# Mamba stage of a decoder: GpSimd takes seven of the 32 products with C, z of batch 1 later, no spare products in the items

## The chip, the cores and the metric

One Trainium2 chip, one core of it. The metric is the device time of one execution in microseconds (us), median of the runs. Engines: TensorE (PE; PEld is its weight load), VectorE (DVE), ScalarE (ACT), GpSimd (POOL), SyncE (SP, which here only issues DMAs).

## What is computed

A decoder layer: a Mamba block, a mixture of experts, a cross-attention, six layers of local attention with feed-forward, and a last norm. The change touches only the Mamba block (B = 2, L = 512, 256 channels, 16 states):

```python
xz = rmsnorm(x) @ in_proj_w
xi, z = split(xz)
xi = silu(causal_conv4(xi) + conv_b)
dbc = xi @ x_proj_w                       # 64 for the step size, 16 for B, 16 for C
delta = softplus(dbc[..., :64] @ dt_proj_w + dt_proj_b)
Bm, Cm = dbc[..., 64:80], dbc[..., 80:96]
A = -exp(A_log)
h = exp(delta * A) * h + (delta * xi) * Bm     # for each of 16 states, along L
y = sum over states of h * Cm
y = (y + D_skip * xi) * silu(z)
out = y @ out_proj_w                      # and the residual is added
```

## The kernel before

**Layout.** Channels lie on the 128 partitions in two halves k = 0, 1; time lies along the free axis. All is fp32. After a front part (norm, convolution as four accumulated products, low-rank projection, step size of batch 0), `build_mamba` works through 32 *items*, item i = 16 b + n being state n of batch b. Every engine has its own written-out program for the items, and semaphores tie them together.

**One item.** SP loads B's row, broadcast to 128 partitions, from DRAM into a ring of four (`b_rows`, L158), once GpSimd has used the row four items earlier. GpSimd multiplies u = delta * x by it (`dbx`, 128x1024, a ring of three, L492), at most three items ahead of the scans. ScalarE makes the decay exp(delta * A) for each half into one of four PSUM banks (`decay`, L315), each once the scan two items back has read its bank. VectorE scans each half (`scan`, L412) into `state` (two buffers), and multiplies the state by C's row (`times_c`, L419, 128x1024) into `hc`, a ring of three. Its order is scan(i, 0), times_c(i - 1), scan(i, 1). TensorE spreads C's row over the partitions by a product with a selection matrix into one PSUM bank (`spread_c`, L194), and adds `hc` into the sum banks by products with the identity (`add_state`, L205). spread_c(i + 1) stands ahead of add_state(i); it waits until times_c(i) has read the bank, and two spare products (`busy`, L170, bf16 zeros) run ahead of it.

**What is threaded between the items.** For batch 1: TensorE's products for z10 and z11 (`gate_proj`, L178) after items 0 and 1, with ScalarE copying x10, x11 (`raw`, L294) after the decays of item 1 and z10, z11 after those of items 2 and 3. x1's SiLU (`activated`, L333 to L341, with a table load before and one after) follows the decays of item 3. Then the low-rank product (`low_rank`, L183) ahead of item 4, rank copy and low part on VectorE (items 6, 7), step size products (items 7, 11), softplus in three ScalarE steps (items 10 to 14), delta on VectorE (`step_sizes`, L404, items 10, 13), u on GpSimd (`step_times_x`, L475, ahead of items 12 and 16). For batch 0: SiLU of z (item 16), skip on VectorE (L423, item 17), gate on GpSimd (L497, item 19), output product (item 20), residual (L427, item 22). Batch 1 ends the same way on VectorE after item 31.

The banks 3 (SPARE), 4 and 5 (the two sums) and 7 (C's row) are shared between these uses. A single bank serves z10, z11, the low-rank product, the step sizes and the output product.

## Time and profile before

| | us |
|---|---|
| median of 3 runs (lowest to highest) | 1226.83 (1225.7 to 1227.47) |
| the profiled execution | 1222.83 |
| its span | 1221.0 |
| busy: PE, DVE, ACT, POOL | 1126.8, 943.2, 845.5, 653.3 |

The page's shares are averages over all stages. The Mamba stage is the first eighth of the span: it ends with the last residual at 158.29 us. In the order of time, a line gives start, length, engine, line of the kernel, what is written from what, and in brackets how long the engine was idle before it and what ended that. The granted clock is TensorE's, 1.00 for 2.4 GHz and 0.50 for 1.2 GHz.

### The profile page before, as it was taken

To read this page: it belongs to the slowest core of one execution; us is meant where nothing else is said; L and a number is where in the kernel's file an instruction comes from. 1 tells how busy PE (TensorE), PEld (TensorE's weight loads), DVE (VectorE), ACT (ScalarE), POOL (GpSimd) and SP (SyncE) were. 2 spreads that over 40 slices of the span, in tenths; PEclk is the share of its full clock that TensorE was granted. 3 is DMA by queue.
4 is the path that set the end of the run, shared out by engine and by line. 5 is a ranking of instruction groups with operands and counts; after the bars stand their busy time and mean duration, and the time that the engine had idled before them with its cause. 6 is when DMAs were issued, how large, how long until landed. Compare 5 with 4: busy or idle time off the path is not lost. (4 is left out here: it accounts for less than half of the span.)

```text
span 1221.0 us, 26331 instructions
## 1 busy us (share of the span) xinstructions
PE 1126.8 (92%) x9600; PEld 718.5 (59%) x9700; DVE 943.2 (77%) x1386; ACT 845.5 (69%) x1344; POOL 653.3 (54%) x527
## 2 busy tenths in 40 slices
PE   9788879999776999999999999999999999999975
PEld 3223248787333766666666676666666666667641
DVE  4699957778455878887888787888888788878843
ACT  5446356665353788688877788688877887787844
POOL 2567424543334765655656566656666565756510
PEclk9899979999886999999999999999999999999998
DMA  4222035100202453345435353445334443534310
GB/s 154 78 61 78 26 54 216 52 26 1 103 1 52 111 156 93 102 118 135 100 96 135 105 127 94 119 104 142 98 100 120 123 122 80 127 94 123 92 52 17
DMA packets 80183, 115.58 MB, mean 95 GB/s; under 512 B 25891, under 2 KB 32482, under 8 KB 79674
## 3 DMA queue, kind: packets, MB, share of 16 engines
q1 hardware_dynamic: 79546, 113.13, 35.0%
q8 instruction: 77, 1.26, 0.4%
q10 hardware_dynamic: 512, 0.80, 0.2%
q14 instruction: 48, 0.39, 0.1%
HBM read 39.28 MB, written 0.66 MB: 33 GB/s over the span
## 5 line engine op out<-in xcount | busy, mean ns | idle before, releaser
L1758 POOL TENSOR_TENSOR st_sq_sum<-h 128x512 f32<-128x512 f32 x96 | 122.2, 1272 | 222.9 <-ACT h L1515 222.2
L1762 POOL TENSOR_TENSOR mo_w<-mo_w,x 128x512 f32<-128x512 f32 x96 | 122.7, 1278 | 101.7 <-DVE x L1633 101.7
L1647 DVE SCALAR_TENSOR_TENSOR st_turned<-banks,mo_w 128x1024 f32<-128x1024 f32 x96 | 117.5, 1224 | 73.0 <-ACT banks L1526 40.7
L1515 ACT ACTIVATE h<-banks 128x512 f32<-128x512 f32 x192 | 114.6, 597 | 70.3 <-PE banks L1358 65.9
L1419 PEld LDWEIGHTS banks<-st_p_blocks,st_vs 128*64 128x64 f32 x1536 | 81.4, 137 | 78.1 <-issue 76.0
L1378 PEld LDWEIGHTS banks<-st_wv,stream 128*128 128x128 f32 x768 | 100.7, 191 | 45.2 <-issue 44.4
L1764 POOL TENSOR_TENSOR mo_w<-mo_w,x 128x512 f32<-128x512 f32 x96 | 122.4, 1275 | 0.0
L1547 ACT ACTIVATE st_p_blocks<-banks 64x512 f32<-64x512 f32 x192 | 112.0, 583 | 3.2 <-PE banks L1407 0.8
L1366 PE MATMUL banks<-st_sq_sum,head_ones 128*128 128x512 f32 x192 | 101.4, 610 | 11.9 <-POOL st_sq_sum L1758 7.7
L1771 POOL TENSOR_TENSOR mo_w<-st_prob,st_ri 128x512 f32<-128x512 f32 x96 | 100.3, 1045 | 15.0 <-DVE st_ri L1733 15.0
L1395 PE MATMUL banks<-st_k_blocks,st_qT 128*32 128x128 f32 x3072 | 104.6, 277 | 1.6 <-DMA st_k_blocks<-st_turned 1.5
L1419 PE MATMUL banks<-st_p_blocks,st_vs 128*64 128x64 f32 x1536 | 99.4, 227 | 6.1 <-ACT st_p_blocks L1547 5.5
L1522 ACT ACTIVATE st_rn<-banks,fill 128x512 f32<-128x512 f32 x96 | 65.8, 685 | 55.5 <-PE banks L1366 55.2
L1378 PE MATMUL banks<-st_wv,stream 128*128 128x128 f32 x768 | 101.2, 275 | 0.0
L1429 PE MATMUL banks<-x,st_wo 128*128 128x512 f32 x192 | 99.3, 599 | 1.8 <-ACT x L1540 1.7
L1354 PE MATMUL banks<-st_y_high,st_w_high 128*128 128x512 f32 x192 | 92.0, 479 | 9.4 <-PEq L1885 4.8
L1419 PE MATMUL banks<-st_p_blocks,st_vn 128*64 128x64 f32 x1536 | 95.7, 222 | 0.0
L1395 PEld LDWEIGHTS banks<-st_k_blocks,st_qT 128*32 128x32 f32 x3072 | 78.6, 110 | 25.9 <-issue 17.4
L492 POOL TENSOR_TENSOR ma_dbx<-ma_u,ma_b_rows 128x1024 f32<-128x1024 f32 x31 | 72.7, 2362 | 28.6 <-DVE ma_state L412 28.5
L1581 ACT ACTIVATE st_prob<-st_prob 128x512 f32<-128x512 f32 x96 | 60.3, 628 | 39.2 <-DVE st_prob L1711 38.4
L412 DVE TENSOR_TENSOR_SCAN ma_state<-banks,ma_dbx 128x512 f32<-128x512 f32 x64 | 75.6, 1207 | 8.4 <-ACT banks L315 6.6
L1419 PEld LDWEIGHTS banks<-st_p_blocks,st_vn 128*64 128x64 f32 x1536 | 81.9, 138 | 0.0
(240 smaller groups left out, 2713.3 us busy)
## 6 DMA issues: line engine op xcount, KB each, us to landing
st_qT<-st_turned SPq DMA_DIRECT2D x192, 128.0 KB, 2.3
st_k_blocks<-st_turned SPq DMA_DIRECT2D x384, 64.0 KB, 2.0
st_vs<-st_vn SPq DMA_DIRECT2D x96, 192.0 KB, 2.5
ma_b_rows<-state_rows SPq DMA_DIRECT2D x32, 256.0 KB, 3.1
st_w_raw<-in_w_qk SPq DMA_DIRECT2D x12, 512.0 KB, 4.9
st_vs<-st_vn SPq DMA_DIRECT2D x96, 48.0 KB, 2.1
mo_w_all<-gate_rows SPq DMA_DIRECT2D x1, 3072.0 KB, 11.8
st_wv<-in_w_v SPq DMA_DIRECT2D x12, 256.0 KB, 2.9
```

The lines of the kernel that those rows point to most:

```text
L1366: mm(NORM_BANK, C["head_ones"], sq_sum[:], start=True, stop=True).then_inc(norm_done.sem, 1)
L1378: last = mm(V_BANK[:, rows], Y[:, b, rows], wv[:, pair, :], start=True, stop=True)
L1395: last = mm(SCORE_BANK[rows].rearrange("p (o h i k) -> p o h i k", o=2, h=2, i=2)[:, odd, :, i, :], qT[:, r, pair, t0:t0 + WIN], k_blocks[ ...
L1419: last = mm(TURN_BANK[rows, P * j:P * j + P].rearrange("p (h o q) -> p h o q", h=2, q=WIN)[:, :, odd, :], (vn if odd else vs)[:, r, j, row ...
L1429: mm(OUT_BANK[b], wo[:, pair, :], oT[:, n % 2, :], start=(pair == 0), stop=(pair == 7)).then_inc(wo_step.sem, 1)
L1515: A(sq[:, part, :], ps[:, part, :], ACT.Square).then_inc(sq_done.sem, 1)
L1547: A(p_blocks[rows, r, half, :], TURN_BANK[rows, :], ACT.Copy).then_inc(pt_copied.sem, 1)
L1647: v.scalar_tensor_tensor(turned[:, h % 4], NORM_BANK.unsqueeze(1).to_broadcast([P, 2, SEQ]), 1e12, cos_part[:, which], ALU.min, ALU.mult). ...
L1758: nc.gpsimd.tensor_tensor(sq_sum[:], sq[:, 0, :], sq[:, 1, :], ALU.add).then_inc(sq_summed.sem, 1)
L1762: nc.gpsimd.tensor_tensor(cos_part[:, which, 0, :], cos_part[:, which, 0, :], sin_part[:, 1, :], ALU.subtract).then_inc(add_done.sem, 1)
L1764: nc.gpsimd.tensor_tensor(cos_part[:, which, 1, :], cos_part[:, which, 1, :], sin_part[:, 0, :], ALU.add).then_inc(add_done.sem, 1)
L1771: nc.gpsimd.tensor_tensor(pn[:, r], prob[:, r], ri[:, r, :].unsqueeze(2).to_broadcast([P, 8, 64]), ALU.mult).then_inc(pn_done.sem, 1)
```

## The change

Seven items, 2, 6, ..., 26 (`BY_POOL`), have their product with C on GpSimd, from SBUF: C's row comes by DMA into the one buffer `c_rows`. For this all 32 rows (B and C) go out to DRAM. GpSimd does the product of item m after dbx of item m + 2. TensorE spreads no C row for these items, and `add_state` and the scans wait for whichever engine made the product (`hc_at`). `state` gets a third buffer, so that scan(i) waits for the product of item i - 3. TensorE's two spare products per item are gone, and ten stand ahead of item 0 instead. The products for z10 and z11 move from items 0 and 1 to 15 and 18, their copies to the decays of items 17 and 20. x1's SiLU, the low-rank product and what follows from it for batch 1 come one item earlier. SiLU of z0 one item earlier, of z1 one later, output product and residual of batch 0 two later. `mag` is no longer separate per batch.

```diff
--- before.py
+++ after.py
@@ -99,14 +99,15 @@
     xc = sb("xc", [P, 2, 2, SEQ])
     dt = sb("dt", [DT_RANK + 1, 2, SEQ])
     bc2 = sb("bc2", [P, 2, SEQ], F32R)
-    mag = sb("mag", [P, 2, 2, SEQ])
+    mag = sb("mag", [P, 2, SEQ])
     delta = sb("delta", [P, 2, 2, SEQ])
     u = sb("u", [P, 2, 2, SEQ])
     still = sb("still", [P, SEQ], BF16)
     a_neg = sb("a_neg", [P, 2, STATES])
     b_rows = sb("b_rows", [P, B_RING, SEQ])
     dbx = sb("dbx", [P, 3, 2, SEQ])
-    state = sb("state", [P, 2, 2, SEQ])
+    state = sb("state", [P, 3, 2, SEQ])
+    c_rows = sb("c_rows", [P, SEQ])
     hc = sb("hc", [P, 3, 2, SEQ])
     gated = sb("gated", [P, 2, 2, SEQ])
 
@@ -122,11 +123,19 @@
     b_flat_done, b_out, b_in = flow("b_flat_done"), flow("b_out"), [flow(f"b_in_{i}") for i in range(B_RING)]
     c_done, decay_done, dbx_done, scan_done, hc_done, sum_done = (flow(n) for n in (
         "c_done", "decay_done", "dbx_done", "scan_done", "hc_done", "sum_done"))
+    pool_hc_done, c_in = flow("pool_hc_done"), flow("c_in")
     gate_step, out_done, h1_done = flow("gate_step"), flow("out_done"), flow("h1_done")
 
     block = ctx.enter_context(nc.Block())
 
     ITEMS = 2 * STATES
+
+    BY_POOL = range(2, ITEMS - 2, 4)
+    BY_DVE = [i for i in range(ITEMS) if i not in BY_POOL]
+
+    def hc_at(i):
+
+        return (pool_hc_done.sem, BY_POOL.index(i) + 1) if i in BY_POOL else (hc_done.sem, BY_DVE.index(i) + 1)
 
     FRONT = {name: i + 1 for i, name in enumerate(("x00", "x01", "z00", "z01", "x10", "x11", "z10", "z11"))}
     RAW = {name: i + 1 for i, name in enumerate(("z00", "z01", "x10", "x11", "z10", "z11"))}
@@ -151,11 +160,16 @@
             b, n = divmod(i, STATES)
             if n == 0:
                 sp.wait_ge(b_flat_done.sem, b + 1)
-                sp.dma_start(d["states"][b], b_flat[64:64 + STATES, b, :]).then_inc(b_out.sem, 16)
+                sp.dma_start(d["states"][b], b_flat[64:64 + 2 * STATES, b, :]).then_inc(b_out.sem, 16)
                 sp.wait_ge(b_out.sem, 16 * (b + 1))
             if i >= B_RING:
                 sp.wait_ge(dbx_done.sem, 2 * (i - B_RING + 1))
-            sp.dma_start(b_rows[:, i % B_RING, :], bass.AP(d["states"].tensor, i * SEQ, [[0, P], [1, SEQ]])).then_inc(b_in[i % B_RING].sem, 16)
+            sp.dma_start(b_rows[:, i % B_RING, :], bass.AP(d["states"].tensor, (2 * STATES * b + n) * SEQ, [[0, P], [1, SEQ]])).then_inc(b_in[i % B_RING].sem, 16)
+            if i in BY_POOL:
+                at = BY_POOL.index(i)
+                if at >= 1:
+                    sp.wait_ge(pool_hc_done.sem, at)
+                sp.dma_start(c_rows[:], bass.AP(d["states"].tensor, (2 * STATES * b + STATES + n) * SEQ, [[0, P], [1, SEQ]])).then_inc(c_in.sem, 16)
 
     @block.tensor
     def _(pe):
@@ -188,14 +202,15 @@
 
         def spread_c(i):
             b, n = divmod(i, STATES)
+            if i in BY_POOL:
+                return
             if i > 0:
-                pe.wait_ge(hc_done.sem, i)
-                busy(2)
+                pe.wait_ge(hc_done.sem, BY_DVE.index(i))
             mm(ps[:, C_BANK, :], select[64:128, n, :], bc2[64:128, b, :], start=True, stop=True).then_inc(c_done.sem, 1)
 
         def add_state(i):
             b, n = divmod(i, STATES)
-            pe.wait_ge(hc_done.sem, i + 1)
+            pe.wait_ge(*hc_at(i))
             if n == 0:
                 if b == 0:
                     pe.wait_ge(raw_done.sem, RAW["x11"])
@@ -239,27 +254,33 @@
         convolved(1, 1)
         pe.wait_ge(C["const_in"].sem, C["const_n"])
         pe.wait_ge(out_in.sem, 16)
+        pe.wait_ge(raw_done.sem, RAW["z01"])
+        for _ in range(10):
+            mm(ps[:, SUM + 1, :], still[:, 0:P], still[:], start=True, stop=True)
         for i in range(ITEMS):
-            if i == 4:
-                pe.wait_ge(raw_done.sem, RAW["z11"])
+            if i == 3:
+                pe.wait_ge(raw_done.sem, RAW["x10"])
                 low_rank(1, SPARE)
-            if i == 7:
+            if i == 6:
                 pe.wait_ge(dt_copied.sem, 2)
                 pe.wait_ge(low_done.sem, 2)
                 pe.wait_ge(b_flat_done.sem, 2)
                 step_size(1, 0, SPARE)
-            if i == 11:
+            if i == 10:
                 pe.wait_ge(delta_done.sem, 3)
                 step_size(1, 1, SPARE)
-            if i == STATES + 4:
+            if i == 15:
                 pe.wait_ge(delta_done.sem, 4)
+                gate_proj(1, 0)
+            if i == 18:
+                pe.wait_ge(raw_done.sem, RAW["z10"])
+                gate_proj(1, 1)
+            if i == 22:
+                pe.wait_ge(raw_done.sem, RAW["z11"])
                 out_proj(0)
             if i + 1 < ITEMS:
                 spread_c(i + 1)
             add_state(i)
-            if i in (0, 1):
-                pe.wait_ge(raw_done.sem, RAW[("x10", "z10")[i]])
-                gate_proj(1, i)
         pe.wait_ge(h1_done.sem, 1)
         out_proj(1)
 
@@ -298,7 +319,7 @@
             A(bc2[64:128, b, :], ps[64:128, bank, :], ACT.Copy).then_inc(high_done.sem, 1)
 
         def flat(b, bank):
-            A(b_flat[64:64 + STATES, b, :], ps[64:64 + STATES, bank, :], ACT.Copy).then_inc(b_flat_done.sem, 1)
+            A(b_flat[64:64 + 2 * STATES, b, :], ps[64:64 + 2 * STATES, bank, :], ACT.Copy).then_inc(b_flat_done.sem, 1)
 
         def decay(i):
             b, n = divmod(i, STATES)
@@ -319,15 +340,15 @@
 
         def magnitude(b, k):
             ac.wait_ge(dtp_done.sem, 2 * b + k + 1)
-            A(mag[:, b, k, :], ps[:, SPARE if b else k, :], ACT.Abs).then_inc(softplus_step.sem, 1)
+            A(mag[:, k, :], ps[:, SPARE if b else k, :], ACT.Abs).then_inc(softplus_step.sem, 1)
 
         def decline(b, k):
             ac.wait_ge(softplus_step.sem, STEP[b, k, "abs"])
-            A(mag[:, b, k, :], mag[:, b, k, :], ACT.Exp, scale=-1.0).then_inc(softplus_step.sem, 1)
+            A(mag[:, k, :], mag[:, k, :], ACT.Exp, scale=-1.0).then_inc(softplus_step.sem, 1)
 
         def log_of(b, k):
             ac.wait_ge(softplus_step.sem, STEP[b, k, "exp"])
-            A(mag[:, b, k, :], mag[:, b, k, :], ACT.Ln, bias=C["one"]).then_inc(softplus_step.sem, 1)
+            A(mag[:, k, :], mag[:, k, :], ACT.Ln, bias=C["one"]).then_inc(softplus_step.sem, 1)
 
         def activated(which, at):
             nc.scalar.preload_act_table_set("silu_and_others")
@@ -357,21 +378,21 @@
             if i == 1:
                 raw("x10")
                 raw("x11")
-            if i in (2, 3):
-                raw(("z10", "z11")[i - 2])
-            if i == 3:
+            if i == 2:
                 activated("x1", "x11")
-            if i == 7:
+            if i == 6:
                 high(1, SPARE)
                 flat(1, SPARE)
+            if i in (9, 12):
+                magnitude(1, i // 12)
+                decline(1, i // 12)
             if i in (10, 13):
-                magnitude(1, i // 13)
-                decline(1, i // 13)
-            if i in (11, 14):
-                log_of(1, i // 14)
-            if i == 16:
+                log_of(1, i // 13)
+            if i == 15:
                 activated("z0", "z01")
-            if i == 23:
+            if i in (17, 20):
+                raw(("z10", "z11")[i // 20])
+            if i == 24:
                 activated("z1", "z11")
 
     @block.vector
@@ -401,22 +422,22 @@
 
         def step_sizes(b, k):
             dv.wait_ge(softplus_step.sem, (4, 6, 9, 12)[2 * b + k])
-            v.scalar_tensor_tensor(delta[:, b, k, :], ps[:, SPARE if b else k, :], 0.0, mag[:, b, k, :], ALU.max, ALU.add).then_inc(delta_done.sem, 1)
+            v.scalar_tensor_tensor(delta[:, b, k, :], ps[:, SPARE if b else k, :], 0.0, mag[:, k, :], ALU.max, ALU.add).then_inc(delta_done.sem, 1)
 
         def scan(i, k):
             j = 2 * i + k
             dv.wait_ge(decay_done.sem, j + 1)
             dv.wait_ge(dbx_done.sem, 2 * i + (k + 1 if i == 0 else 2))
-            if i >= 2:
-                dv.wait_ge(hc_done.sem, i - 1)
-            v.tensor_tensor_scan(state[:, i % 2, k, :], ps[:, DECAY[j % 4], :], dbx[:, i % 3, k, :], 0.0, ALU.mult, ALU.add).then_inc(scan_done.sem, 1)
+            if i >= 3:
+                dv.wait_ge(*hc_at(i - 3))
+            v.tensor_tensor_scan(state[:, i % 3, k, :], ps[:, DECAY[j % 4], :], dbx[:, i % 3, k, :], 0.0, ALU.mult, ALU.add).then_inc(scan_done.sem, 1)
 
         def times_c(i):
             dv.wait_ge(scan_done.sem, 2 * i + 2)
-            dv.wait_ge(c_done.sem, i + 1)
+            dv.wait_ge(c_done.sem, BY_DVE.index(i) + 1)
             if i >= 3:
                 dv.wait_ge(sum_done.sem, 2 * (i - 2))
-            v.tensor_tensor(hc[:, i % 3], state[:, i % 2], ps[:, C_BANK, :].unsqueeze(1).to_broadcast([P, 2, SEQ]), ALU.mult).then_inc(hc_done.sem, 1)
+            v.tensor_tensor(hc[:, i % 3], state[:, i % 3], ps[:, C_BANK, :].unsqueeze(1).to_broadcast([P, 2, SEQ]), ALU.mult).then_inc(hc_done.sem, 1)
 
         def skip(b, k):
             dv.wait_ge(sum_done.sem, 2 * STATES * (b + 1) - 1 + k)
@@ -437,21 +458,21 @@
             v.tensor_tensor(u[:, 0, k, :], delta[:, 0, k, :], xc[:, 0, k, :], ALU.mult).then_inc(u_done.sem, 1)
         for i in range(ITEMS):
             scan(i, 0)
-            if i >= 1:
+            if i >= 1 and i - 1 in BY_DVE:
                 times_c(i - 1)
             scan(i, 1)
+            if i == 5:
+                rank_copy(1, SPARE)
             if i == 6:
-                rank_copy(1, SPARE)
-            if i == 7:
                 low_part(1, SPARE)
-            if i == 10:
+            if i == 9:
                 step_sizes(1, 0)
-            if i == 13:
+            if i == 12:
                 step_sizes(1, 1)
             if i == STATES + 1:
                 for k in range(2):
                     skip(0, k)
-            if i == STATES + 6:
+            if i == STATES + 8:
                 residual(0)
         times_c(ITEMS - 1)
         for k in range(2):
@@ -476,10 +497,11 @@
 
         for i in range(ITEMS):
             b, n = divmod(i, STATES)
-            if i == 12:
+            if i == 11:
                 step_times_x(0)
-            if i == 16:
+            if i == 15:
                 step_times_x(1)
+            if i == STATES:
                 pool.wait_ge(u_done.sem, 4)
             pool.wait_ge(b_in[i % B_RING].sem, 16 * (i // B_RING + 1))
             if i >= 3:
@@ -490,6 +512,13 @@
                     nc.gpsimd.tensor_tensor(dbx[:, 0, k, :], u[:, 0, k, :], b_rows[:, 0, :], ALU.mult).then_inc(dbx_done.sem, 1)
             else:
                 nc.gpsimd.tensor_tensor(dbx[:, i % 3], u[:, b], b_rows[:, i % B_RING, :].unsqueeze(1).to_broadcast([P, 2, SEQ]), ALU.mult).then_inc(dbx_done.sem, 2)
+            if i - 2 in BY_POOL:
+                at, m = BY_POOL.index(i - 2), i - 2
+                pool.wait_ge(scan_done.sem, 2 * m + 2)
+                pool.wait_ge(c_in.sem, 16 * (at + 1))
+                if m >= 3:
+                    pool.wait_ge(sum_done.sem, 2 * (m - 2))
+                nc.gpsimd.tensor_tensor(hc[:, m % 3], state[:, m % 3], c_rows[:].unsqueeze(1).to_broadcast([P, 2, SEQ]), ALU.mult).then_inc(pool_hc_done.sem, 1)
             if i == STATES + 3:
                 pool.wait_ge(gate_step.sem, 2)
                 pool.wait_ge(silu_done.sem, 5)
@@ -1834,7 +1863,7 @@
 
 
     d = {**d, "line": nc.dram_tensor("bias_line", (HEADS, SPAN), F32).ap(),
-         "states": nc.dram_tensor("state_rows", (BATCH, STATES, SEQ), F32).ap(),
+         "states": nc.dram_tensor("state_rows", (BATCH, 2 * STATES, SEQ), F32).ap(),
          "gates": nc.dram_tensor("gate_rows", (EXPERTS, BATCH, SEQ), F32).ap()}
     with ExitStack() as ctx:
         def sb(name, shape, dt=F32):
```

## Rows read from the trace of the kernel before

**Rows 1.** Mamba by stretch: PE, PEld, DVE, ACT, POOL busy us, granted clock, DMA share, GB/s

```profile
48.00:60.00 12.00, 8.98 (x17) 3.45 (x18) 8.74 (x8) 6.75 (x11) 4.71 (x2) 0.72 0.20 58
84.00:96.00 12.00, 9.93 (x24) 3.60 (x25) 12.00 (x13) 8.52 (x11) 10.48 (x6) 1.00 0.29 97
```

**Rows 2.** Groups by line, 20 to 170 us: busy us, mean ns, idle before

```profile
L412 DVE TENSOR_TENSOR_SCAN ma_state<-banks,ma_dbx 128x512 f32<-128x512 f32 x64 | 75.6, 1207 | 8.4 <-ACT banks L315 6.6 <-POOL ma_dbx L492 1.5 <-POOL ma_dbx L490 0.3
...
L315 ACT ACTIVATE banks<-ma_delta,ma_a_neg 128x512 f32<-128x512 f32 x64 | 43.2, 686 | 43.3 <-DVE ma_state L412 43.0 <-DVE ma_delta L404 0.2
L419 DVE TENSOR_TENSOR ma_hc<-ma_state,banks 128x1024 f32<-128x1024 f32 x32 | 38.2, 1195 | 2.7 <-issue 2.6
```

**Rows 3.** VectorE in order of time: start, length, instruction, idle before it

```profile
40.93 1.22 DVE L412 TENSOR_TENSOR_SCAN ma_state<-banks,ma_dbx 128x512 f32<-128x512 f32 x1 [2.39 <-ACT banks L315]
...
48.62 1.22 DVE L412 TENSOR_TENSOR_SCAN ma_state<-banks,ma_dbx 128x512 f32<-128x512 f32 x1 [4.22 <-ACT banks L315]
...
59.20 1.22 DVE L419 TENSOR_TENSOR ma_hc<-ma_state,banks 128x1024 f32<-128x1024 f32 x1 [2.64 <-issue]
...
132.75 2.33 DVE L412 TENSOR_TENSOR_SCAN ma_state<-banks,ma_dbx 128x512 f32<-128x512 f32 x2
135.00 1.19 DVE L419 TENSOR_TENSOR ma_hc<-ma_state,banks 128x1024 f32<-128x1024 f32 x1
```

**Rows 4.** ScalarE in order of time, the same columns

```profile
31.67 1.29 ACT L315 ACTIVATE banks<-ma_delta,ma_a_neg 128x512 f32<-128x512 f32 x2
39.72 0.60 ACT L294 ACTIVATE ma_sz<-banks 128x512 f32<-128x512 f32 x1 [6.75 <-PE banks L178]
...
43.96 1.28 ACT L333 ACT_TABLE_LOAD   x1
45.25 1.33 ACT L337 ACTIVATE ma_xc<-ma_xc,ma_chan 128x512 f32<-128x512 f32 x2
```

**Rows 5.** TensorE in order of time, the same columns

```profile
34.41 0.38 PE L170 MATMUL banks<-ma_still 128*128 128x512 bf16 x1 [3.27 <-DVE ma_hc L419]
...
51.02 1.03 PE L170 MATMUL banks<-ma_still 128*128 128x512 bf16 x2 [4.74 <-DVE ma_hc L419]
51.98 0.79 PE L194 MATMUL banks<-ma_bc,ma_select 64*128 64x512 f32 x1
52.70 3.78 PE L205 MATMUL banks<-ma_hc,ident 128*128 128x512 f32 x4
56.28 1.97 PE L183 MATMUL banks<-ma_xc,ma_proj_w 128*128 128x512 f32 x4
58.08 0.59 PE L170 MATMUL banks<-ma_still 128*128 128x512 bf16 x2
...
72.97 1.98 PE L205 MATMUL banks<-ma_hc,ident 128*128 128x512 f32 x4
```

**Rows 6.** GpSimd in order of time, the same columns

```profile
29.26 9.30 POOL L492 TENSOR_TENSOR ma_dbx<-ma_u,ma_b_rows 128x1024 f32<-128x1024 f32 x4
...
103.02 2.50 POOL L497 TENSOR_TENSOR ma_gated<-ma_gated,ma_sz 128x512 f32<-128x512 f32 x2 [2.21 <-DVE ma_gated L423]
...
140.85 2.36 POOL L492 TENSOR_TENSOR ma_dbx<-ma_u,ma_b_rows 128x1024 f32<-128x1024 f32 x1 [1.00 <-DVE ma_state L412]
```

**Rows 7.** VectorE in order of time, its other work: step size, skips

```profile
76.37 0.66 DVE L404 SCALAR_TENSOR_TENSOR ma_delta<-banks,ma_mag 128x512 f32<-128x512 f32 x1
...
101.57 1.38 DVE L423 SCALAR_TENSOR_TENSOR ma_gated<-ma_xc,ma_chan,banks 128x512 f32<-128x512 f32 x2
...
153.53 0.75 DVE L423 SCALAR_TENSOR_TENSOR ma_gated<-ma_xc,ma_chan,banks 128x512 f32<-128x512 f32 x1 [1.49 <-PE banks L205]
```

**Rows 8.** DMA of the B rows: burst at 22.9 us, then 83 to 140 us

```profile
DMA to landing us min/median/max: 3.1/3.8/4.2
...
DMA to landing us min/median/max: 3.0/3.1/3.3
```

**Rows 9.** TensorE in a later stretch: busy us, granted clock, DMA, GB/s

```profile
315.00:321.00 6.00, 3.11 (x6) 1.00 0.00 0
```

## The prediction

> **What bounds the kernel now.** I began with the table of busy time by stage. Only the Mamba stage, to 158.3 us of a 1221.0 us span, contains lines of the diff. In it VectorE is busy 12.00 of 12.00 us from 84 us on, but 8.74 of 12.00 us from 48 to 60 us [rows 1]. The groups by line say what fills it: 64 scans (1207 ns) and 32 products with C (1195 ns) [rows 2]. VectorE's order of time gives the pace: two scans start at 132.75 and the product at 135.00, though their record is 2.33 long, so a scan holds VectorE for 1.125 us and a record ends 0.085 after the next instruction may start; the product of 1.19 then holds it for 1.11, and an item, two scans and a product, takes 3.36 us [rows 3]. The three holes are in the same view: idle 2.39 us before 40.93, 4.22 before 48.62 and 2.64 before 59.20. Each is counted from the record's end, 0.085 late, so the holes cost 9.25 + 0.25 = 9.5 us [rows 3]. ScalarE's order of time explains two: it sits 6.75 us waiting for TensorE's z10 product before it may copy z10, and the decays of item 3 queue behind; then z11's copy, a table load of 1.28, two SiLUs of 1.33 together and a table load of 1.28 all stand ahead of the decays of item 4 [rows 4]. The third is TensorE's: at half clock C's row takes 0.72 us and two sum products 3.58, from start to start (51.98, 52.70, 56.28), then the low-rank product and two spare products stand ahead of C's row for item 5 [rows 5]. GpSimd isn't the bound: 2.36 us of work, 1.00 us of waiting in an item; four without a wait take 9.30, 2.33 from start to start [rows 6].
>
> **The change, part by part.** "Item" is a pair (batch, state), 0 to 31.
>
> *Products moved.* Items 2, 6, ..., 26, seven of the 32, lose VectorE's product: 7 x 1.11 = 7.8 us off VectorE's path. Each puts one 128x1024 product of two SBUF operands on GpSimd, for which I take that of its own product dbx, 2.36 us (2.33 from start to start) [rows 6]. Bounds: no reason makes it shorter; slower I can't see from this trace, since the type, shape and kinds of operands are the same.
>
> *Holes at the front.* z10 and z11 leave items 0 to 3 of TensorE and ScalarE, and the SiLU of x1 moves ahead by one item. Laid out anew: decays of item 2 end at 33.0 as now [rows 4]; load, two SiLUs, load take 3.9, to 36.9; decay of item 3 is there at 37.6, and VectorE wants it at 38.45 (40.93 less the hole of 2.48). So both ScalarE holes go; margin 0.85. The third goes with the second, whose 4.74 us of idle TensorE stand ahead of the half clock [rows 5]. What is late next is, first, TensorE: the product with C of item 2 on GpSimd starts when dbx of item 4 is done (38.6 as now [rows 6]) and ends at 41.0, the two sums then take 1.83 (1.98 at full clock, less the overlap of 0.2 that the slow ones show [rows 5]), the low-rank product, four passes of the same form, 1.8, and C's row of item 4 some 0.45: 45.1, and VectorE wants it at 45.1. No margin, even with TensorE at full clock. Second GpSimd: dbx of item 5 ends at 43.3, wanted at 44.0. So 9.5 us go, with 0 to 0.5 coming back here.
>
> *GpSimd's queue later.* Over four items GpSimd has 5 x 2.33 = 11.65, VectorE 8 x 1.125 + 3 x 1.11 = 12.33, so GpSimd keeps up by 0.7 only, and every other thing on it is felt. It waits for the new step size before item 11 and from then on works without a pause. From dbx 11 to dbx 13 it then has dbx, product, dbx = 6.99, while VectorE needs four scans, one product and a step size of 0.6 [rows 7] = 6.2: a stall of 0.75. From 13 to 17 GpSimd has 5 x 2.33 + 1.23 for u = 12.9 against 12.33: 0.55. From 17 to 21 it has 11.65 + 2.46 for the gate [rows 6] and 0.2 of waiting for the first skip, 14.3, against 12.33 + 1.3 for the two skips [rows 7]: 0.65. After that VectorE is the slower one again. Together +1.95 us. Bounds 1 to 4: it is a difference of nearly equal sums, and 0.1 us more per GpSimd instruction would already be 2 us over the 20 in a row.
>
> *C's row by DMA.* Seven transfers of 256 KB are queued on SP between the B rows, and from item 6 on SP waits for the last GpSimd product with C. Behind that wait stand the B rows of the next two items, in a burst of three. A single B row lands in 3.0 to 3.2 us; of the burst of four at the start the last takes 4.2 [rows 8]. The B row of item 7 is issued at 41.5, so it lands by 45.6 at the latest, and GpSimd wants it at 45.6; that of items 19 and 23 has the same margin. Cost 0, at most 0.3 each for three, under 1 us. The first transfer out carries 32 rows of 2 KB in place of 16. The nearest rows are those of 256 KB in 3.1 us; a transfer 32 KB longer should land within 0.3 us of the old one. Taken as 0, since the first scan waits for VectorE's own u, bounds -0.1 to +0.3.
>
> *Spare products removed.* TensorE loses two per item. At the end C's row for item 31 no longer has 0.53 of them ahead of it, so the last sums start as soon as their product is there: the 1.49 us wait before the skip [rows 7] becomes 1.05: -0.45. What the removal does to TensorE's clock is a rival below. Ten spare products before the loop fill 31.1 to 33.3, where TensorE is idle for 3.27 us [rows 5]: free.
>
> *Hidden, each with its cover.* z10 and z11 later (TensorE has about 1 us free in an item, ScalarE the 3.36 less two decays of 0.69 [rows 2]); the smaller magnitude buffer (its two users are far apart); the third state buffer (GpSimd's product is done 3.2 us before the scan that overwrites its state). SiLU of z0 and z1 on ScalarE with its loads: 3.6 us against 5.6 until the next decay is wanted. If that cover were gone, each would cost some 1 us.
>
> *Sum.* -9.5 - 7.8 - 0.45 + 1.95 = -15.8 us. Profiled: span 1221.0 becomes 1205.2 and 1222.83 becomes 1207.0. That run was 4.0 us under the median; the stage after Mamba is untouched, so I take the same 15.8 off the median: **1211.0**.
>
> **The rivals.**
> *A fall of TensorE's clock.* After a pause of 3.27 us (31.14 to 34.41) and one of 4.74 us TensorE ran at half clock, 1.2 GHz: the granted clock is 0.72 in the mean from 48 to 60 us [rows 1], two spare products took 1.03 us at 51.02. They took 0.59 again at 58.08, after seven microseconds of work without a pause [rows 5]. In the new order TensorE idles about 1.1 us in most items, 25 to 30% in all, and, waiting for GpSimd's product of items 10 and 14, 2.9 and 2.6 us at a stretch. Against a fall: from 315 to 321 it was busy 3.11 of 6.00 us at a clock of 1.00 [rows 9]. Price of one fall: at half clock an item of TensorE takes 0.72 + 3.58 = 4.3 against 3.36, and C's row has 2.2 us of room, so VectorE feels only the third such item: 0 to 1.5 us. At the low-rank product, where there is no room, it is 3, and at the last sums and output products 3. One fall at a dear place: 1214.
> *Repeated falls.* If the clock fell once for each of the seven GpSimd items, at the 1.3 us in the middle of these prices, this is 9 us: 1220. Rows speak on both sides: half idle from 315 to 321 us it didn't fall, after 3.27 us at a stretch it did. The Trainium skill (TensorE: Matmul & The Clock Gate, "A second HAM failure mode: psum-queue depth-cycling") speaks for this rival and so against the change: a TensorE that idles briefly but often between groups of products can swing between its two clocks. By that rule the time is this 1220; the trace agrees only in part.
> *GpSimd becomes the bound.* If its product with C or the hand-over costs 0.3 more than dbx, 2.66 + 4 x 2.36 = 12.1 leaves no room, and each of the disturbed cycles costs 0.3 to 0.5, with late B rows on top: +2 to +5, 1215.
> *Part of the front stays.* If the order before item 5 goes otherwise than laid out, and only 4 of the 9.5 us go: 1216.
> *Slower than before.* The low clock holds: four items then take 4 x 3.58 + 3 x 0.72 = 16.5 us of TensorE against the 13.4 of VectorE now. Over the stage 8 x 3.1 = 24.6 more, less the 9.5 of the front: 1242. It decides from where the low clock holds for four of the eight groups of four items (15.8 / (16.5 - 12.3) = 3.8). Against it: at half clock TensorE has no pause left, and that is the state out of which the clock rose before 58.08.
> *It doesn't do what it says.* If GpSimd waits so that VectorE waits for it at every moved product, nothing of the 7.8 is gained: 1219.
>
> **How the numbers follow.** Forecast as summed 0.63; one dear or several cheap clock falls 0.13, repeated falls 0.05; GpSimd as bound 0.09; front partly kept 0.04; nothing from the moved products 0.02; slower 0.03; something that leaves it within 0.2% (about 2.5 us, what a measurement here can tell from no change) 0.01. The unknown terms of the sum give 1208.5 to 1213; the range reaches on into the falls and GpSimd, to 1216, which leaves out less than 2 in 10. Low end 1208: all new stalls absent (1209) and the 1 us by which the runs shown differ. Faster 0.96, same 0.01, slower 0.03.
>
> **What would show it.** Right: no VectorE hole over 1 us between 33 and 60 us; 25 products by VectorE and 7 by GpSimd of 2.36; the last residual ending near 142.5 in place of 158.29 us; holes of 0.4 to 0.8 before the scans of items 11, 13, 17 and 21, released by dbx; GpSimd without a pause from about 62 to 113 us; the clock at 1.00 in the items. Wrong: a granted clock of 0.50 inside the items with VectorE waiting for C's row; GpSimd products over 2.4 us; GpSimd waiting for a B row; or a stage after 158 us that takes a different time, which my sum has at nothing.

## The result, and the profile after

| kernel | median us (lowest to highest, runs) | ratio to before (95% interval) | profiled: us, span |
|---|---|---|---|
| before | 1226.58 (1225.7 to 1227.47, 4) | | 1222.83, 1221.0 |
| changed | 1211.22 (1207.73 to 1213.08, 4) | 0.9865 (0.985 to 0.9881) | 1207.73, 1205.9 |

The prediction was 1211.0 us, its profiled form 1207.0 with a span of 1205.2. Below, three measures of a profiled execution are used for every kernel: the start of the first scan, the *items* (from there to the end of the last residual) and the *rest* (from there to the end of the span).

| | first scan | items | rest |
|---|---|---|---|
| before | 27.88 | 130.41 | 1062.71 |
| changed | 29.04 | 114.28 | 1062.58 |

So 16.1 us went from the items, 1.2 came in ahead of them, and the rest is the same in these two executions. Of the 1.2, 0.9 is there already at 8 us, where the loads that everything begins with landed later. The other 0.2 comes at the first scan: in the kernel before it waited for VectorE's second product for u (26.18, 1.78 long), here for GpSimd's first product (27.33, 1.61 long). The sum had nothing for either. In the executions below the first scan starts between 27.9 and 28.6 us, whatever the edit.

VectorE of the changed kernel in order of time (the columns of rows 3), its holes and the end:

```profile
38.20 4.56 DVE L433 TENSOR_TENSOR_SCAN ma_state<-banks,ma_dbx 128x512 f32<-128x512 f32 x4
...
46.12 1.22 DVE L440 TENSOR_TENSOR ma_hc<-ma_state,banks 128x1024 f32<-128x1024 f32 x1
...
66.57 3.54 DVE L433 TENSOR_TENSOR_SCAN ma_state<-banks,ma_dbx 128x512 f32<-128x512 f32 x3 [0.37 <-issue]
...
73.51 1.22 DVE L433 TENSOR_TENSOR_SCAN ma_state<-banks,ma_dbx 128x512 f32<-128x512 f32 x1 [0.58 <-ACT banks L336]
74.93 1.22 DVE L440 TENSOR_TENSOR ma_hc<-ma_state,banks 128x1024 f32<-128x1024 f32 x1 [0.19 <-PE banks L209]
...
98.00 1.22 DVE L440 TENSOR_TENSOR ma_hc<-ma_state,banks 128x1024 f32<-128x1024 f32 x1 [0.20 <-DVE ma_state L433]
...
100.67 1.22 DVE L433 TENSOR_TENSOR_SCAN ma_state<-banks,ma_dbx 128x512 f32<-128x512 f32 x1 [0.32 <-issue]
...
138.55 0.75 DVE L444 SCALAR_TENSOR_TENSOR ma_gated<-ma_xc,ma_chan,banks 128x512 f32<-128x512 f32 x1 [1.22 <-PE banks L220]
...
142.63 0.69 DVE L448 TENSOR_TENSOR h<-banks,x 128x512 f32<-128x512 f32 x1 [1.22 <-PE banks L225]
```

The last line is the last residual; it ends at 143.32, where it was 158.29. The three front holes [rows 3] are gone: from 38.20 on scans follow each other, and what remains there is a product that starts 0.08 us later than the engine could (46.12 in place of 46.04), where the prediction had no margin. The later holes are small: 0.37 us before the scan of item 11, 0.58 before the first scan of item 13, 0.19 before the product of item 12, which waits for C's row, 0.20 before the product of item 19, which waits for C's row too, and 0.32 before item 21; the two scans of 85.01 (not shown) are 0.19 longer together than their like, which is item 17. The wait before the skip is 1.22, from 1.49 [rows 7].

ScalarE, table load, SiLUs of x1, table load, then four decays:

```profile
33.93 1.28 ACT L354 ACT_TABLE_LOAD   x1
35.22 1.33 ACT L358 ACTIVATE ma_xc<-ma_xc,ma_chan 128x512 f32<-128x512 f32 x2
36.58 1.28 ACT L362 ACT_TABLE_LOAD   x1
37.87 2.52 ACT L336 ACTIVATE banks<-ma_delta,ma_a_neg 128x512 f32<-128x512 f32 x4
```

Loads and SiLUs end at 37.87, one microsecond later than laid out, since the whole kernel is one microsecond late. GpSimd in order of time:

```profile
47.12 4.67 POOL L514 TENSOR_TENSOR ma_dbx<-ma_u,ma_b_rows 128x1024 f32<-128x1024 f32 x2 [0.64 <-DMA ma_b_rows<-state_rows]
...
62.90 1.26 POOL L496 TENSOR_TENSOR ma_u<-ma_delta,ma_xc 128x512 f32<-128x512 f32 x1 [3.42 <-DVE ma_delta L425]
...
68.75 2.36 POOL L521 TENSOR_TENSOR ma_hc<-ma_state,ma_c_rows 128x1024 f32<-128x1024 f32 x1
...
91.16 2.50 POOL L526 TENSOR_TENSOR ma_gated<-ma_gated,ma_sz 128x512 f32<-128x512 f32 x2 [0.29 <-DVE ma_gated L444]
```

The product with C (L521) takes 2.34 to 2.38 us, as long as dbx [rows 6]. From 62.90 to 117 us the only pause is the 0.29 us at 91.16, for the first skip. At 47.12 it waited 0.64 us for a B row. The loads, KB each and median us from issue to landing:

```profile
ma_b_rows<-state_rows SPq DMA_DIRECT2D x32, 256.0 KB, 3.6
ma_c_rows<-state_rows SPq DMA_DIRECT2D x7, 256.0 KB, 3.3
```

Their median is 3.6 us, where it was 3.1 in the kernel before: the wait for GpSimd's products sends B rows out in bursts of three. TensorE in order of time, and all engines by stretch (the columns of rows 1):

```profile
71.16 2.95 PE L220 MATMUL banks<-ma_hc,ident 128*128 128x512 f32 x4 [2.77 <-POOL ma_hc L521]
...
83.96 1.98 PE L220 MATMUL banks<-ma_hc,ident 128*128 128x512 f32 x4 [2.00 <-POOL ma_hc L521]
...
91.22 5.39 PE L220 MATMUL banks<-ma_hc,ident 128*128 128x512 f32 x8 [1.65 <-DVE ma_gated L444]
```

```profile
28.00:48.00 20.00, 17.16 (x44) 6.55 (x42) 17.85 (x16) 15.15 (x23) 19.30 (x10) 1.00 0.42 121
48.00:60.00 12.00, 9.89 (x21) 3.43 (x21) 11.94 (x13) 6.35 (x10) 10.77 (x5) 1.00 0.33 100
72.00:84.00 12.00, 9.86 (x19) 3.26 (x17) 11.23 (x12) 8.01 (x10) 12.00 (x7) 0.86 0.39 115
84.00:96.00 12.00, 10.35 (x19) 3.92 (x20) 11.91 (x12) 4.68 (x8) 11.71 (x7) 0.86 0.32 110
```

TensorE's clock was 1.00 to 72 us, but fell twice later: after the pauses of 2.77 and of 2.00 and 1.65 us behind GpSimd's products and the first skip, four sum products took 2.95 instead of 1.98, and eight 5.39 instead of 3.95. It read 0.51 from 72 to 75 and from 93 to 96 us. C's row was late by it twice, by the 0.19 and the 0.20 us above.

### The profile page after: what moved, and what is told of

Read it like the earlier page. It is cut to its first block and busy times, and to the rows that moved or that the text cites. A ratio compares the mean times of both kernels' runs of the same rounds, so it can differ in the third digit from the quotient of the medians.

```text
span 1205.9 us, 26320 instructions
## 1 busy us (share of the span) xinstructions
PE 1110.2 (92%) x9641; PEld 709.4 (59%) x9641; DVE 935.4 (78%) x1379; ACT 844.9 (70%) x1344; POOL 669.2 (55%) x534
## 5 line engine op out<-in xcount | busy, mean ns | idle before, releaser
L220 PE MATMUL banks<-ma_hc,ident 128*128 128x512 f32 x128 | 66.2, 643 | 14.9 <-POOL ma_hc L521 7.5
```

## Experiments

Each was timed against the kernel before on its own chip, of three; the median of before was 1225.6 for e1 to e4, 1225.6 for e7 and e9 to e11, and 1226.5 for e5, e6, e8 and e12. Ratios can be compared across these groups, and medians to about 1 us. "After" in a diff is the changed kernel.

| kernel | median us (lowest to highest) | ratio to before (95% interval) | items | rest |
|---|---|---|---|---|
| e1 changed, no products on GpSimd | 1216.60 (1213.20 to 1217.37) | 0.9922 (0.9908 to 0.9936) | 120.40 | 1067.15 |
| e2 before, products moved alone | 1225.85 (1224.25 to 1232.56) | 1.0011 (0.9995 to 1.0027) | 129.07 | 1069.90 |
| e3 changed, spare products back | 1212.85 (1212.26 to 1213.43) | 0.9897 (0.9883 to 0.9911) | 116.02 | 1067.35 |
| e4 changed, items 4 to 28 | 1210.21 (1205.66 to 1210.66) | 0.9865 (0.9847 to 0.9883) | 113.26 | 1067.17 |
| e5 changed, ten products | 1224.71 (1223.24 to 1229.21) | 0.9992 (0.9979 to 1.0006) | 129.05 | 1065.50 |
| e6 before, no spare products | 1225.34 (1219.54 to 1227.99) | 0.9988 (0.9972 to 1.0004) | 125.95 | 1066.97 |
| e7 changed, two pauses filled | 1211.08 (1209.01 to 1212.15) | 0.9873 (0.9855 to 0.9892) | 114.29 | 1068.07 |
| e8 before, z late alone | 1218.82 (1216.54 to 1221.90) | 0.9944 (0.9925 to 0.9964) | 121.65 | 1065.01 |
| e9 e2 without spare products | 1219.59 (1218.78 to 1221.49) | 0.9950 (0.9934 to 0.9967) | 124.84 | 1064.64 |
| e10 changed, eight products | 1211.79 (1208.40 to 1212.34) | 0.9874 (0.9854 to 0.9893) | 112.77 | 1069.57 |
| e11 changed, spare products after Mamba | 1211.34 (1208.29 to 1214.39) | 0.9881 (0.9860 to 0.9902) | 114.28 | 1065.90 |
| e12 e4 and e11 together | 1208.36 (1206.86 to 1212.32) | 0.9861 (0.9839 to 0.9884) | 113.56 | 1064.67 |

The last column warns of how to read the second: in stages that no edit but e11 and e12 touched, profiled executions differ by up to 7 us. The items are the sharper measure, but of one execution each.

**e1: what the moved products are worth.**

```diff
-    BY_POOL = range(2, ITEMS - 2, 4)
+    BY_POOL = range(0)
```

> The changed kernel, but all 32 products with C are VectorE's; order, spare products and buffers as changed. Theory (the terms add up): VectorE gets back 7 x 1.11 = 7.8 us, the stalls behind GpSimd's queue (1.5 us between items 13 and 21) go, so 1211.2 + 7.8 - 1.5 = 1217.5 us, and no VectorE hole over 0.4 us between 33 and 135 us. Rival (GpSimd's products gain nothing, all came from the front): 1211 to 1213. Second rival (the front's holes go only because the products are moved): the holes of 2 to 4 us before 60 us come back, over 1221.

The items took 120.40, 6.1 us more than in the changed kernel; 7.8 - 1.5 = 6.3 was expected. The median rose by 5.4, by the ratios it is 7.0. The front holes did not come back; this is VectorE's only hole over 0.15 us after the start and ahead of the last skip:

```profile
67.92 1.22 DVE L433 TENSOR_TENSOR_SCAN ma_state<-banks,ma_dbx 128x512 f32<-128x512 f32 x1 [0.37 <-issue]
```

So the front doesn't need the products, and in the new order the products are worth 6.1 us net.

**e2: the products alone, in the old order.** The edit is the diff without its parts on z, on x1's SiLU and the low-rank chain, and on spare products.

```diff
+    BY_POOL = range(2, ITEMS - 2, 4)
...
-    state = sb("state", [P, 2, 2, SEQ])
+    state = sb("state", [P, 3, 2, SEQ])
```

> The kernel before, with the seven products on GpSimd, C's row by DMA and the third state buffer alone; z, SiLU of x1, low-rank product and spare products stay where they were. Theory: the three front holes stay (9.5 us) and the spare products too (0.45), and GpSimd's queue stalls VectorE by some 3 us where it has u to compute, so 1226.6 - 7.8 + 3 = 1222 us (1220 to 1223). Rival (front and products each give their full share independently): 1226.6 - 7.8 = 1218.8. Rival (products do nothing): 1226.6.

Nothing was gained, against the 4.6 us expected, and the items are 1.3 us shorter, not 4.8. The profiled execution is 4.3 us over the median, and its rest is the longest of all. The front holes stood (2.38, 4.30, 2.84), and three new ones of over 1 us came, which VectorE's order of time has:

```profile
78.85 1.22 DVE L428 TENSOR_TENSOR_SCAN ma_state<-banks,ma_dbx 128x512 f32<-128x512 f32 x1 [1.49 <-ACT banks L331]
...
83.47 1.22 DVE L428 TENSOR_TENSOR_SCAN ma_state<-banks,ma_dbx 128x512 f32<-128x512 f32 x1 [1.15 <-POOL ma_dbx L508]
87.61 1.22 DVE L435 TENSOR_TENSOR ma_hc<-ma_state,banks 128x1024 f32<-128x1024 f32 x1 [2.92 <-PE banks L210]
```

TensorE at the same place:

```profile
81.12 3.78 PE L221 MATMUL banks<-ma_hc,ident 128*128 128x512 f32 x4 [4.83 <-POOL ma_hc L515]
84.69 1.92 PE L201 MATMUL banks<-ma_dt,ma_dt_w 65*128 65x512 f32 x2
```

In the old order GpSimd waits for the step size ahead of dbx 12, and the product of item 10 comes behind dbx 12. TensorE has to wait 4.83 us for it, its clock falls, the two sums take 3.78, and the step-size product (1.92) stands ahead of C's row, for which VectorE waits 2.92. In the new order the wait for the step size stands ahead of dbx 11, two GpSimd instructions before that product is due. So in this trace 5.6 of the 7.8 us are lost at the one place where the step size arrives. That "one item earlier", which I had costed at nothing, is what avoids it is read from the two traces; no run has only that edit.

**e9: e2 without spare products.**

```diff
                 pe.wait_ge(hc_done.sem, BY_DVE.index(i))
-                busy(2)
```

> The kernel before with the seven products on GpSimd, as in the run where nothing was gained, and now without the two spare products per item. That run had a hole of 2.92 us on VectorE behind TensorE at half clock (78 to 87 us) and 1.15 to 1.49 us behind GpSimd. Theory (with spare products TensorE has no room when it starts late behind GpSimd and the clock falls as well; without them it has): the 2.92 us go to under 1, the wait before the skip falls by 0.3, items 129.1 to about 126 us, time 1225.9 - 3 = 1222.5. Rival (GpSimd's queue alone eats the gain): 1225 to 1226, holes of the same sum in other places.

The median fell by 6.3 us, twice what was expected, and the items by 4.2, but not for the reason given. The hole behind TensorE at half clock stayed:

```profile
75.58 1.22 DVE L427 TENSOR_TENSOR_SCAN ma_state<-banks,ma_dbx 128x512 f32<-128x512 f32 x1 [1.50 <-ACT banks L330]
...
80.19 1.22 DVE L427 TENSOR_TENSOR_SCAN ma_state<-banks,ma_dbx 128x512 f32<-128x512 f32 x1 [1.14 <-POOL ma_dbx L507]
84.16 1.22 DVE L434 TENSOR_TENSOR ma_hc<-ma_state,banks 128x1024 f32<-128x1024 f32 x1 [2.75 <-PE banks L209]
```

What went is in the front: of the three holes the first is gone and the third is 1.52 (from 2.84). That called for e6.

**e6: the kernel before without spare products.**

```diff
             if i > 0:
                 pe.wait_ge(hc_done.sem, i)
-                busy(2)
```

> The kernel before without the two spare products per item, nothing else. Removing them from the kernel with the products alone on GpSimd gained 6.3 us, where 3 were expected. Theory A (they matter only at half clock and where TensorE is late): the third front hole (2.64 us) shrinks to 1.5, the wait before the skip by 0.3, items 130.4 to 127.5 us, time 1222.5. Theory B (they also make the z10 product late, so the first front hole of 2.39 us is partly theirs): items 125 us, time 1220, and that much of the change's gain is the removal of spare products, not the move of z. Theory C (they are paid for by the clock): no change or slower, 1226.

In the profiled execution the holes are those that theory B named: ScalarE waited 4.45 us for z10, where it was 6.75 [rows 4], the first front hole is gone, the third is 1.46 and the items are 4.5 us shorter. ScalarE, then VectorE:

```profile
37.59 0.60 ACT L293 ACTIVATE ma_sz<-banks 128x512 f32<-128x512 f32 x1 [4.45 <-PE banks L178]
```

```profile
46.17 1.22 DVE L411 TENSOR_TENSOR_SCAN ma_state<-banks,ma_dbx 128x512 f32<-128x512 f32 x1 [3.89 <-ACT banks L314]
...
55.57 1.22 DVE L418 TENSOR_TENSOR ma_hc<-ma_state,banks 128x1024 f32<-128x1024 f32 x1 [1.46 <-issue]
```

But spare products are the smaller part of it. ScalarE gets z10 2.1 us sooner, and ahead of z10 the spare products hold TensorE for 0.31 us (34.41 to 34.72 [rows 5]). About 1.7 us of it, an estimate from the starts and lengths below, is TensorE's clock, which fell at this place in the kernel before (0.50 from 36 to 39 us) and didn't in e6 (1.00). The four sum products and z10's, before, then e6:

```profile
35.14 3.00 PE L205 MATMUL banks<-ma_hc,ident 128*128 128x512 f32 x4
37.94 1.75 PE L178 MATMUL banks<-ma_hn,ma_in_w 128*128 128x512 f32 x2
```

```profile
34.71 1.98 PE L204 MATMUL banks<-ma_hc,ident 128*128 128x512 f32 x4
36.53 1.02 PE L178 MATMUL banks<-ma_hn,ma_in_w 128*128 128x512 f32 x2
```

e2 and e9 differ in the same way: the same four sum products took 3.63 us in e2 and 1.98 in e9. Whether the removal of spare products is what kept the clock up isn't shown: the pause ahead of these products was 3.27 us in before and 3.00 in e6, but 3.27 also in e8, which has the spare products and where the clock stayed at 1.00. What the third hole lost is the spare products' own: in the kernel before four of them stand between item 3's product and C's row for item 5 and hold TensorE for 1.5 us [rows 5].

The median moved by only 1.1 us, with an interval that takes in 1. In the profiled execution the rest was 4.3 us longer than in that of before. Whether the other executions had the shorter items isn't to be seen, so the worth of this edit by itself stays open between 0 and 4.5 us. e9 and e6 differ by the moved products and what they need, and here the two measures disagree: the items by 1.1 us, the ratios (0.9950 and 0.9988, intervals apart) by 4.7 us. So with spare products the time shows that the moved products are worth nothing in the old order (e2). Without spare products only one profile says so, and the time speaks against it.

**e8: z late, and what hangs on it.** With the cut shown go SiLU of z1, output product and residual of batch 0, as in the change, and the low-rank product waits for x11 in place of z11.

```diff
-            if i in (0, 1):
-                pe.wait_ge(raw_done.sem, RAW[("x10", "z10")[i]])
-                gate_proj(1, i)
...
-            if i in (2, 3):
-                raw(("z10", "z11")[i - 2])
+            if i in (17, 20):
+                raw(("z10", "z11")[i // 20])
```

> The kernel before with only the products for z10 and z11, their copies, the SiLU of z1 and the output product of batch 0 moved as in the change; the SiLU of x1 stays after item 3, spare products and all products with C stay. Theory (the front holes are the queueing behind z10 and z11): the holes of 2.39, 4.22 and 2.64 us go to under 0.5 each, items 130.4 to 121 us, time 1225.6 - 9.5 = 1216. Rival (the table loads ahead of item 4's decays are what costs the 4.22, and only moving the SiLU earlier helps): that hole stays, 1221 to 1222.

The items fell by 8.8 us to 121.65, the ratio is 0.9944. VectorE runs through the front, and its first hole over 0.3 us after that is one that the kernel before has too, before item 12 (0.38 us at 80.78):

```profile
37.48 2.33 DVE L415 TENSOR_TENSOR_SCAN ma_state<-banks,ma_dbx 128x512 f32<-128x512 f32 x2
...
71.53 1.22 DVE L415 TENSOR_TENSOR_SCAN ma_state<-banks,ma_dbx 128x512 f32<-128x512 f32 x1 [0.37 <-POOL ma_dbx L495]
```

The SiLU of x1 with its two table loads is still behind item 3, and costs nothing there. The 4.22 us hole was z's, not the table loads': with z out of the way ScalarE starts the loads early enough. So the front's 9.5 us are nearly all from the move of z (8.8 in the items, 7.7 by the median), and the earlier SiLU isn't needed for them. What the clock would have cost in front of z10 is in these 8.8 (see e6).

**e3: spare products back in the changed kernel.**

```diff
                 pe.wait_ge(hc_done.sem, BY_DVE.index(i))
+                busy(2)
```

> The changed kernel with two spare products ahead of each of VectorE's C rows again. Theory (the spare products cost by TensorE's queue, and the clock hardly matters): +0.4 at the end, +0.5 at the low-rank product and +0.3 twice where an extra product stands ahead of a C row, 1211.2 + 1.5 = 1212.7 us. Rival (their removal lets the clock fall from 72 and 92 us on, which costs more than they do): the granted clock is 1.00 throughout the items and the time is 1209 to 1210; the runs lie within 2 us of one another instead of 5.

Items +1.7, median +1.6, as expected to 0.2. But half of it is at a place that wasn't expected: next to 0.43 at the low-rank product and 0.28 at the end, a C row came 1.05 us late (0.19 in the changed kernel), behind four sum products at half clock, for the clock fell between 69 and 72 us in spite of the spare products:

```profile
45.63 1.22 DVE L441 TENSOR_TENSOR ma_hc<-ma_state,banks 128x1024 f32<-128x1024 f32 x1 [0.43 <-DVE ma_state L434]
...
75.30 1.22 DVE L441 TENSOR_TENSOR ma_hc<-ma_state,banks 128x1024 f32<-128x1024 f32 x1 [1.05 <-PE banks L210]
```

**e7: the pauses filled, at three places.**

```diff
         def add_state(i):
             b, n = divmod(i, STATES)
+            for _ in range({10: 9, 14: 8, 18: 3}.get(i, 0)):
+                mm(ps[:, SUM + 1, :], still[:, 0:P], still[:], start=False, stop=False)
             pe.wait_ge(*hc_at(i))
```

> The changed kernel with 9, 8 and 3 spare products (zeros, added into a sum bank, so the sums stay the same) where TensorE waits for GpSimd's product of items 10, 14 and 18. In the changed kernel's trace the clock read 0.51 from 72 to 75 and from 93 to 96 us, after pauses of 2.8 and 2.0 us. Theory (these falls are nearly hidden): the clock stays at 1.00 up to 90 us, VectorE's holes shrink by 0.2 us only, from the first scan to the last residual it is 114.3 us as before within 0.4, time 1211 (1210 to 1212). Rival (the falls are what costs in the items): 2 us or more less, 112 us for the items.

The clock stayed at 1.00 through the items, in the stretches where it had fallen:

```profile
71.00:74.00 3.00, 3.00 (x8) 1.00 0.59 197
...
93.00:96.00 3.00, 2.84 (x8) 1.00 0.00 0
```

and the items took 114.29 against 114.28. So the falls in the items cost nothing net. VectorE's order of time says why: C's row is in time now, but the holes before items 17 and 21, behind GpSimd, are 0.39 and 0.65 where they were 0.19 and 0.32. What VectorE had lost to TensorE it now loses to GpSimd's queue.

**e4, e10, e5: which items, and how many.**

```diff
-    BY_POOL = range(2, ITEMS - 2, 4)
+    BY_POOL = range(4, ITEMS - 2, 4)            # e4
+    BY_POOL = (1, 5, 8, 12, 16, 20, 25, 29)     # e10
+    BY_POOL = range(2, ITEMS - 2, 3)            # e5
```

> The changed kernel with GpSimd's seven products at items 4, 8, ..., 28 instead of 2, 6, ..., 26. Theory (the stalls before items 13, 17 and 21 are GpSimd's queue: its product of item 10 falls into the stretch where it also computes u, its product of item 18 beside the gate): now GpSimd has its product of item 8 done before it waits for the step size, and the 1.5 us of holes go, together with part of the late B row before item 5: 1211.2 - 2.0 = 1209.2 us, no hole over 0.4 us after 60 us. Rival (the stalls are set by the totals of both engines, not by the place): no change, 1211. Rival (the holes there are TensorE's clock): holes stay, 1211 to 1213.

> The changed kernel with eight of GpSimd's products, at items 1, 5, 8, 12, 16, 20, 25, 29, placed where laying out its queue leaves it room. Theory (what bounds the gain is where GpSimd is idle, not how many products it has): VectorE loses one more product, 1.1 us, and the holes after 60 us go: from the first scan to the last residual 114.3 - 2.8 = 111.5 us, time 1208.4. Rival (GpSimd is full with seven): its queue holds up scans in new places, items 114 us or more, time 1211 or more.

> The changed kernel with ten products on GpSimd, items 2, 5, ..., 29. Over three items GpSimd then has 4 x 2.33 = 9.3 us against 6 x 1.125 + 2 x 1.11 = 9.0 on VectorE. Theory (GpSimd is near its bound with seven and becomes the bound with ten): VectorE waits for dbx or for GpSimd's product in most groups, and with u and the gate on top the gain of the moved products is gone: from the first scan to the last residual 120 us (114.3 with seven, 120.4 with none), time 1217. Rival (GpSimd has room, each product is worth 1.11 us): 111 us, 1208.

e4: items 113.26, 1.0 shorter where 2.0 were expected. The holes before items 13, 17 and 21 are gone, so they were GpSimd's queue; new ones of 0.21 and 0.65 came, behind a C row. TensorE had paused for 1.55 us behind GpSimd's product, its clock fell, and at 107.59 the output product stands ahead of the C row. VectorE, then TensorE (busy, clock, DMA share, GB/s):

```profile
109.98 1.22 DVE L440 TENSOR_TENSOR ma_hc<-ma_state,banks 128x1024 f32<-128x1024 f32 x1 [0.65 <-DVE ma_state L433]
...
102.00:105.00 3.00, 3.00 (x5) 0.58 0.48 182
```

By the median e4 can't be told from the change. e10: items 112.77, 1.5 shorter where 2.8 were expected, with a new hole of 0.94 where the low-rank product stands ahead of a C row. Here too the clock had fallen, after a pause of 2.09 us behind GpSimd's product. TensorE, then VectorE:

```profile
39.00:42.00 3.00, 3.00 (x5) 0.58 0.69 227
...
46.74 1.22 DVE L440 TENSOR_TENSOR ma_hc<-ma_state,banks 128x1024 f32<-128x1024 f32 x1 [0.94 <-DVE ma_state L433]
```

So a fall that costs nothing in the changed kernel comes with holes of 0.65 and 0.94 us where an extra product of TensorE follows it; without the fall these kernels weren't run.

e5: items 129.05, the median nearly that of before. Expected was the loss of the products' gain (120); in fact it is 8.7 more. Some of its holes:

```profile
59.11 1.22 DVE L440 TENSOR_TENSOR ma_hc<-ma_state,banks 128x1024 f32<-128x1024 f32 x1 [2.33 <-PE banks L209]
...
85.85 1.22 DVE L433 TENSOR_TENSOR_SCAN ma_state<-banks,ma_dbx 128x512 f32<-128x512 f32 x1 [1.44 <-ACT banks L336]
...
149.21 1.22 DVE L440 TENSOR_TENSOR ma_hc<-ma_state,banks 128x1024 f32<-128x1024 f32 x1 [3.12 <-issue]
```

With ten products GpSimd is late everywhere, TensorE then gets its sums in lumps, the clock fell six times between 51 and 150 us, and VectorE waits for C's row as well as for dbx. The loss is larger than the count of GpSimd's instructions says; how much of it is the clock was not separated.

**e11, e12: the clock at the start of the next stage.**

```diff
+        spare(12)
         pe.wait_ge(loaded.sem, 48)
...
+        spare(4)
...
+        spare(10)
```

> The changed kernel with spare products in the first 14 us of the stage after Mamba, where TensorE idles for 4.0 us and then ran at clock 0.50 for most of 147 to 161 us: 12 before its first product, 4 and 10 later, into a bank that is written anew afterwards. The time from the last residual to the end differed by 4.6 us between profiled executions (1062.6 and 1067.2) while nothing in those stages was changed. Theory (this difference, and with it most of the scatter of 1207.7 to 1213.1, is the clock at the start of that stage): clock 1.00 from 144 to 161 us, the rest of the kernel at or under 1061, time 1207 (1206 to 1208.5), runs within 2 us. Rival (the scatter arises later, in the cross-attention or the six layers, or the start of the stage waits for GpSimd and ScalarE anyway): 1210 to 1212 and the same scatter.

> The changed kernel with GpSimd's products at items 4, 8, ..., 28 and spare products at the start of the stage after Mamba, the two steps that shortened their stretch by 1.0 and by about 1.3 us. If the two gains add up and the scatter of the later stages is the same for all: 1211.2 - 2.3 = 1209. If the gain at the start of the stage after Mamba is swallowed by what it waits for later: 1210 to 1211.

e11 against the changed kernel, TensorE alone (busy, clock, DMA share, GB/s), e11 first:

```profile
146.00:149.00 3.00, 3.00 (x9) 1.00 0.47 131
...
155.00:158.00 3.00, 3.00 (x11) 0.69 0.06 14
```

```profile
146.00:149.00 3.00, 2.42 (x4) 0.69 0.42 114
...
155.00:158.00 3.00, 1.83 (x4) 0.50 0.00 0
```

The clock was at 1.00 until 152 us, where it had been until 146, and VectorE's first product of the experts' hidden layer came 1.0 us sooner after the last residual (18.1 against 19.1 us). The median didn't move and the scatter stayed at 6 us: my theory of the scatter is wrong. It arises in several places. From the last residual to the first writing of `st_turned` in the six layers the profiled executions took 218.6 to 223.7 us. Within the six layers, from GpSimd's first sum of squares to its last, they took 782.9 (changed) to 786.8 us (e3). What makes one execution differ there from the next was not found. e12 came out at 1208.36, near the 1209 expected if both gains add up. But its items (113.56) are no shorter than e4's, it too has a hole of 0.97 behind a C row near 110 us, and its interval overlaps the change's: no version is shown to be faster than the change.

## Why the prediction was right, and where not

The total was right (1211.22 for 1211.0), and so were its large terms.

- *Front holes, -9.5.* Right in size. The reason given named two causes, z and the earlier SiLU; e8 shows that z alone brings 8.8. What the prediction left out is the clock in front of z10: after the pause of 3.27 us TensorE ran at half clock there, and where it didn't (e6, e9) the first of the three holes is absent with z10 in its old place. The cover found for TensorE ("no margin" at C's row of item 4) was exact: a hole of 0.08 there, 0.43 with spare products (e3), and 0.94 with other items, at half clock (e10).
- *Products, -7.8, and GpSimd's queue, +1.95.* Net 5.85; e1 measured 6.1 in the items. For the 0.75, 0.55 and 0.65 laid out at items 13, 17 and 21 there are 0.58, 0.19 and 0.32, and 0.59, 0.39 and 0.65 with the clock kept up (e7); the 0.37 before item 11 was there before (0.38, before item 12). That they are GpSimd's queue is shown by e4. What I missed is that this term hangs on the order around it: in the old one the same products gave 1.3 us in the items and nothing in the time (e2).
- *Spare products, -0.45.* The mis-sized term. The wait before the skip fell by 0.27, not 0.45, but e3 gives 1.7 us for all of them: I had costed only the end, at a place where TensorE is the last to finish, and not those places in the middle where TensorE runs late, behind an extra product (0.35) or at half clock (0.86, in the one execution profiled).
- *Clock.* "At 1.00 in the items" was wrong: two falls, at a place and after pauses that the rival named (2.9 and 2.6 us laid out, 2.77 and 2.00 measured). Its price, 0 to 1.5 us, was 0 net (e7): C's row is ready 1.6 us before VectorE wants it (125.42 for 127.03) where nothing else is in the way, and the 0.4 us that it came late GpSimd's queue would have taken. Where that room is used up, by a late GpSimd product in e2 or an extra TensorE product in e4 and e10, there are holes of 2.92, 0.65 and 0.94 us. The Trainium skill (TensorE: Matmul & The Clock Gate, "A second HAM failure mode: psum-queue depth-cycling") says that short, frequent idling makes the clock swing and throughput suffer. The trace agrees with the first half (clock 0.86 in the mean from 72 to 96 us) and, for TensorE's own products, with the second (2.95 us for 1.98); the stage did not suffer by it (items 114.28, and 114.29 in e7).
- *C's row by DMA.* GpSimd waited 0.64 us for a B row, more than the 0.3 allowed, and behind it VectorE lost nothing: the dbx that it delayed, of item 7, was done by 49.5 us and wanted at 53.18.
- *The untouched stages.* The sum had them at nothing, which the two profiled executions bear out to 0.13 us. But they scatter by 7 us between executions, and the two that were profiled lay under their medians by nearly the same, 3.7 and 3.5 us. So the agreement to 0.2 us in the total is partly luck; the start, 1.2 us late, is in it too. The items alone, 16.1 us shorter where 15.8 were laid out, are the fairer test.

## What to carry to other kernels

Lay out each engine's queue with the durations of the trace, for the changed order, and not only the engine that is relieved: the three answers that mattered (no hole at the front, 1 to 2 us of new holes, where the margins are thin) came from that. When an engine takes over work that others wait for, look first at what stands ahead of it in its queue: the same seven products were worth 6 us in one order and nothing in another (e2). Here GpSimd paid with 11.65 us of work to VectorE's 12.33 (seven products) and lost everything with 9.3 to 9.0 (ten); eight, placed away from its other duties, shortened the items by another 1.5 us, which the time doesn't show. And look at the other engine's clock after each new pause: whether a fall costs anything depends on what stands behind it.
